# A router's rows turned by DMA transposes instead of TensorE, and a new order at the end of the attention

## The reference

```python
x = x + tanh(g_xattn[0]) * xattn(layernorm(x), ctx, ctx, ...)      # scores are abs(q k / 4), then softmax
x = x + tanh(g_ffn[0]) * ffn(layernorm(x), ...)

def ffn(x, w_router, w1, b1, w2, b2):
    xf = x.reshape(-1, 256)
    logits = xf @ w_router                                         # [4096, 8]
    probs = softmax(logits)
    topk_w, topk_idx = top_k(probs, 2)
    weights = sum(topk_w[..., None] * one_hot(topk_idx, 8), axis=1)
    h = gelu(einsum('te,ieh->tih', xf, w1) + b1)                   # 8 experts, 256 -> 1024
    out = einsum('tih,ihe->tie', h, w2) + b2                       # 1024 -> 256
    return sum(out * weights[..., None], axis=1)
```

## Time and profile before

| | |
|---|---|
| median of 3 runs | 665.48 us (664.07 to 665.98) |
| the profiled execution's own time | 665.24 us |
| its span, first to last instruction | 663.4 us |
| busy: PE / DVE / ACT / POOL | 638.7 / 459.6 / 334.2 / 312.5 us |
| mean granted TensorE clock | 0.982 of full speed |
| attention with router | from about 20 to 250 us |
| its end, mixed with the first expert tiles | from about 250 to 288 us |
| expert tiles of 256 rows, then of 128 | to 529 us, then to the end |

### The profile page before, as it was taken

The page is one execution under the profiler, slowest core; times in us unless marked ns, Lnnn a source line. Parts: engine busy times, 40 slices in busy tenths (PEclk is TensorE's granted clock), DMA queues, the critical chain, the costliest instruction groups (busy, mean ns, idle before and its releaser), DMA issues.

```text
span 663.4 us, 20913 instructions
## 1 busy us (share of the span) xinstructions
PE 638.7 (96%) x6637; PEld 565.5 (85%) x6638; DVE 459.6 (69%) x1298; ACT 334.2 (50%) x741; POOL 312.5 (47%) x420
## 2 busy tenths in 40 slices
PE   7899999999999998889999999999999999999992
PEld 6699999999999988778888888888888888888871
DVE  5688888888888885579756556564655647777772
ACT  4678778877887764532423333242332424444441
POOL 7323577777667553873443333243332434333332
PEclk9999999999999988799999999999999999999997
DMA  6143445554454463334764333333333334443322
GB/s 205 46 158 122 129 157 170 170 164 146 148 187 133 142 164 131 106 69 74 139 92 67 50 48 56 57 51 51 50 55 54 44 56 59 51 54 55 53 33 24
DMA packets 89157, 63.37 MB, mean 96 GB/s; under 512 B 51489, under 2 KB 84775, under 8 KB 88935
## 3 DMA queue, kind: packets, MB, share of 16 engines
q1 hardware_dynamic: 75519, 43.95, 25.6%
q0 software_dynamic: 13440, 18.14, 16.7%
q10 hardware_dynamic: 104, 0.04, 0.0%
HBM read 28.08 MB, written 24.63 MB: 79 GB/s over the span
## 4 chain that ended last, share of the span: by engine, by line
PE 52%; DVE 2%; POOL 2%; issue 1%; DMA 1%; ACT 0%; POOLq 0%; DVEq 0%; ACTq 0%
PE banks L1700 20%; PE banks L1683 19%; PE banks L1718 7%; PE banks L1732 7%; DMA out_dram<-prob_t,meta 1%; POOL routed L813 1%; DVE prob L1270 0%; POOL l_exp L794 0%; DVE v_area L1272 0%; ACT stage L970 0%; POOLq L676 0%; DVE prob_t L1287 0%; DVE prob_t L1283 0%; PE banks L1653 0%; POOL rstd L767 0%
## 5 line engine op out<-in xcount | busy, mean ns | idle before, releaser
L961 ACT ACTIVATE stage<-banks,bias_t 128x256 f32<-128x256 f32 x200 | 83.8, 470 | 166.3 <-PE banks L1683 166.2
L1683 PE MATMUL banks<-x_t,w_hi 128*128 128x256 f16 x800 | 135.6, 276 | 0.0
L1700 PE MATMUL banks<-w,prob 128*128 x800 | 132.4, 273 | 0.6 <-DVE v_area L1272 0.6
L850 POOL DMA_INDIRECT out_dram<-prob_t,meta x46 | 75.4, 1640 | 98.5 <-DVE prob_t L1262 86.7
L1683 PE MATMUL banks<-x_t,w_lo 128*128 128x256 f16 x400 | 110.6, 276 | 0.0
L1700 PE MATMUL banks<-w,v_area 128*128 x400 | 109.1, 273 | 0.0
L1683 PEld LDWEIGHTS banks<-x_t,w_hi 128*128 x800 | 79.1, 99 | 10.0
L1700 PEld LDWEIGHTS banks<-w,prob 128*128 128x128 f16 x800 | 78.0, 98 | 10.0 <-issue 0.8
L970 ACT ACTIVATE stage<-banks,bias_t 128x128 f32<-128x128 f32 x168 | 52.6, 363 | 66.8 <-PE banks L1718 66.5
L813 POOL DMA_INDIRECT routed<-row,pos x64 | 71.0, 1109 | 27.9 <-issue 14.7
L1612 PEld LDWEIGHTS banks<-v_area,prob_t 128*128 128x128 f32 x640 | 74.0, 192 | 4.3 <-DVE attn L1093 0.7
(11 more groups left out here) (244 smaller groups left out, 1262.3 us busy)
## 6 DMA issues: line engine op xcount, KB each, us to landing
stage<-in_L_ffn_w_dram SPq DMA_DIRECT2D x32, 512.0 KB, 4.3
x_in<-in_x_dram SPq DMA_DIRECT2D x16, 256.0 KB, 3.7
x_res<-in_x_dram SPq DMA_DIRECT2D x16, 256.0 KB, 4.1
out_dram<-x_res SPq DMA_DIRECT2D x16, 256.0 KB, 2.7
routed<-pad_rows SPq DMA_DIRECT2D x9, 265.0 KB
out_dram<-prob_t,meta POOLq DMA_INDIRECT x67, 3.8
routed<-row,pos POOLq DMA_INDIRECT x64, 2.8
arena<-in_L_ffn_b_dram SPq DMA_DIRECT2D x1, 1024.0 KB, 5.4
```

Of the source, the lines that this page charges most:

```text
L850: pool.indirect_dma_start(out[:, :], bass.IndirectOffsetOnAxis(ap=meta_of(j, pj)[:, b, E:E + 1].bitcast(U32), axis=0), y[:, pj, b], None, ...
L961: ins = act.activation(hid[:, c], H[:, q, c % PER * SLOTS:(c % PER + 1) * SLOTS], ACT.Gelu_apprx_tanh, bias=k.bias_t[:, bass.ds(e * HC + c ...
L1683: mm = pe.matmul(H[:, q, c % PER * SLOTS:(c % PER + 1) * SLOTS], w[:, bass.ds(e, 1), i, c * P:(c + 1) * P].rearrange("p a n -> p (a n)"), ...
L1700: mm = pe.matmul(Y[pj][:, b * D:(b + 1) * D], h[:, pj, c, b * P:(b + 1) * P], w[:, bass.ds(e, 1), c, :].rearrange("p a n -> p (a n)"), sta ...
```

## The change

For pairs 0 to 12 (`j < LAST_PAIRS`, 13 pairs) the router's rows are no longer turned by TensorE. SP issues two DMA transposes per pair, one per tile, from the fp16 halves in `row` (SBUF) to `rows_t` (SBUF), once both halves are written. `router_logits` then makes three fp16 products per chunk (high x high, high x low, low x high) with the router's weights, which are split into `router_hi` and `router_lo` once. It stands behind `turn_normalised` now. ACT's copy falls away for these pairs, and `copy_rows` and `turn_rows` stay for pairs 13 to 15, each with rows in a buffer of its own (`last_rows`, `x_in`), so that only the copy of pair 13 waits for a low half, that of pair 12.

Besides: the semaphore `router` counts 9 operations and `shared` the last three, `mask` and `l_shift` have two buffers, the padding rows are made at the end of the attention in the memory `turned` and written to DRAM later, `ident_bf` is a strided view of the fp32 identity, and the lists at the end of the attention are ordered anew on PE, ACT and DVE.

```diff
 # SP
                         sp.dma_start(x_res[:, (j - 1) % 2], x_rows[j - 1]).then_inc(x_res_ld[(j - 1) % 2], 16)
+                    if 0 <= j - 3 < LAST_PAIRS:
+                        turn_rows(j - 3)
+
+                def turn_rows(j):
+                    ready(sp, row_hi, j)
+                    ready(sp, row_lo, j)
+                    ready(sp, logit_ps, j - 1)
+                    for tile in range(2):
+                        sp.dma_start_transpose(rows_t[:, :, tile * P:(tile + 1) * P],
+                                               row[:, j % ROWS_HELD, tile, 0:D].bitcast(F16)).then_inc(rows_ld, 16)
...
 # ACT
                     ready(act, factors2, j, FACTOR_OPS[1])
-                    ready(act, logit_ps, j - 1)
+                    if j < LAST_PAIRS:
+                        ready(act, row_lo, j - 1)
+                    elif j == LAST_PAIRS:
+                        ready(act, q_ps, PAIRS - 1)
+                    else:
+                        ready(act, norm1, PAIRS - 1, 2)
...
                 def copy_rows(j):
-                    ready(act, x2t_ps, j)
-                    ready(act, row_lo, j)
+                    ready(act, x2t_ps, j - LAST_PAIRS)
+                    if j == LAST_PAIRS:
+                        ready(act, row_lo, j - 1)
...
-                    if exists(j - 3):
-                        copy_rows(j - 3)
...
-                e = expert(act, 0)
                 act.wait_ge(w_lo, 2 * PAIRS)
-                gelu(0, e, 0)
-                normalise_row(PAIRS - 2)
+                gelu(0, first, 0)
+                gelu(0, first, 1)
+                gelu(0, first, 2)
+                copy_rows(PAIRS - 2)
+                gelu(0, first, 3)
                 high_row(PAIRS - 2)
-                gelu(0, e, 1)
-                copy_rows(PAIRS - 2)
-                gelu(0, e, 2)
                 normalise_row(PAIRS - 1)
+                gelu(1, second, 0)
+                copy_rows(PAIRS - 1)
+                gelu(1, second, 1)
                 high_row(PAIRS - 1)
-                gelu(0, e, 3)
-                copy_rows(PAIRS - 1)
...
 # DVE, end of the attention
                 split_hidden(0, 0, 0)
-                low_row(PAIRS - 2)
+                split_hidden(0, 0, 1)
+                place_rows(PAIRS - 3)
+                shares(PAIRS - 3)
+                low_row(PAIRS - 3)
                 route(PAIRS - 2, 1)
                 choose(PAIRS - 2)
...
                 split_hidden(1, 1, 0)
                 place_rows(PAIRS - 1)
-                for q in range(1, HID_BANKS):
-                    split_hidden(1, 1, q)
+                split_hidden(1, 1, 1)
+                shares(PAIRS - 2)
+                low_row(PAIRS - 1)
+                split_hidden(1, 1, 2)
+                split_hidden(1, 1, 3)
+                finish_rows(0, 0, 0)
+                for q in range(HID_BANKS):
+                    split_hidden(2, 0, q)
                 shares(PAIRS - 1)
...
 # PE
                 def router_logits(j):
-                    ready(pe, x2t_sb, j)
                     ready(pe, places, j - 1, PLACE_OPS, 1)
+                    if j < LAST_PAIRS:
+                        ready(pe, router_halves, 0, 2)
+                        ready(pe, rows_ld, j, 32)
+                        for tile in range(2):
+                            n = 0
+                            for c in range(KC):
+                                for x, w in ((c, router_hi), (c, router_lo), (KC + c, router_hi)):
+                                    mm = pe.matmul(ROUTE[:, tile * E:(tile + 1) * E], rows_t[:, x, tile * P:(tile + 1) * P],
+                                                   w[:, c], start=(n == 0), stop=(n == 3 * KC - 1))
+                                    n += 1
+                        mm.then_inc(logit_ps, 1)
+                        return
+                    ready(pe, x2t_sb, j - LAST_PAIRS)
...
-                    if exists(j - 3):
-                        turn_rows(j - 3)
                     if exists(j - 2):
                         project_attention(j - 2)
+                    if j == PAIRS - 1:
+                        early_experts.extend(expert(pe, tile) for tile in range(2))
+                    if exists(j + 2):
+                        turn_normalised(j + 2)
                     if exists(j - 3):
                         router_logits(j - 3)
-                    if exists(j + 2):
-                        turn_normalised(j + 2)
...
+                first_layer(0, 0, 0, first, 0)
                 router_logits(PAIRS - 3)
                 turn_attention(PAIRS - 1)
-                first_layer(0, 0, 0, first, 0)
+                first_layer(0, 0, 0, first, 1)
                 project_attention(PAIRS - 1)
+                first_layer(0, 0, 0, first, 2)
                 ranks(PAIRS - 3)
-                first_layer(0, 0, 0, first, 1)
                 turn_rows(PAIRS - 2)
-                first_layer(0, 0, 0, first, 2)
+                first_layer(0, 0, 0, first, 3)
                 router_logits(PAIRS - 2)
-                first_layer(0, 0, 0, first, 3)
+                first_layer(1, 0, 1, second, 0)
+                first_layer(1, 0, 1, second, 1)
                 ranks(PAIRS - 2)
                 turn_rows(PAIRS - 1)
-                first_layer(1, 0, 1, second, 0)
-                first_layer(1, 0, 1, second, 1)
-                router_logits(PAIRS - 1)
                 first_layer(1, 0, 1, second, 2)
                 first_layer(1, 0, 1, second, 3)
+                router_logits(PAIRS - 1)
```

More of the change, by code:

```diff
@@ L544, in main_phase @@
         best_f = sb("best_f", [P, 2, 2])
-        mask = sb("mask", [P, 2, 2, E])
+        mask = sb("mask", [P, 2, 2, 2, E])
         weighed = sb("weighed", [P, 2, 2, E])
@@ L647, in small_meta, with normed @@
             return meta[:, p + 2 * (1 - b), 0]
+        def normed(j):
+            if j < LAST_PAIRS:
+                return x2_rows
+            return last_rows if j == LAST_PAIRS else x_in[:, j % 2]
         def row_halves(j):
@@ L1825, in _ @@
                 last = TILES - 1
-                first, second = expert(pe, 0), expert(pe, 1)
+                first, second = early_experts
                 score_banks_free(TILES)
```

137 lines of the change are left out of this document (73 added, 64 removed).

## The result

| | before | after |
|---|---|---|
| median | 665.6 us (664.07 to 665.98, 4 runs) | **676.48 us** (676.12 to 677.06, 4 runs) |
| ratio, 95% interval | | 1.0169 [1.0151, 1.0186] |
| the profiled execution's own time, span | 665.24, 663.4 us | 677.06, 675.2 us |
| mean granted TensorE clock | 0.982 | 0.974 |

A forecast was written before the change was run, and what follows sets the result against it. PE was taken to bound the kernel, each pair costing what PE issues. Pairs with the new wait +10.0, clock falls +13.6 and the end of the attention -8.0 gave +15.6 us on 665.24: 681 us, range 652 to 701.

The forecast's parts named there:

- Work that leaves PE, 0.94 us a pair: In each pair, fp32 transposes and logits (1.26 us) give way to 12 fp16 products (0.32 us): 13 pairs, 12.2 us less.
- The wait, 1.71 us a pair: Before the logits PE waits for the second DMA transpose, landing at 8.93 us; with PE's saving, +10.0 us over 13 pairs.
- the prediction's count: Time within a pair, counted from the end of the query projection on PE, where the attention's transposes begin.
- rival 3: Transposes collide with POOL's four scatters a pair and land at 4.5 us; wait 3.01 us, 706 us in all; chance 0.10.
- rival 1: Rows nearly in time: second transpose lands 2.1 us after its issue, 0.61 us waited a pair; 656 us; chance 0.24.
- DVE can't do those earlier: DVE's low halves of the rows cannot move forward, since operations before them hang on the same pair's query projection.
- the ring: Projection, ACT, DVE, SP, DMA, logits, then probabilities, scores, values, ranks, next projection: the wait comes back every pair.
- The clock, 8 falls of 1.7 us, +13.6 us: PE's granted clock falls behind the new wait in 8 of 13 pairs, at 1.7 us each: +13.6 us.
- Rival 2: The wait before the logits comes but PE's clock holds: +10.0 - 8.0, 667 us; chance 0.16.
- The end, -8.0 us: End of the attention: 4.6 of 5.0 us of PE's waits for ACT's copy and 3.4 us of clock falls go.
- SP's other issues at nothing: SP's rows out, x in and weight loads behind the transposes wait for DVE until 8.42 us anyway; costed at nothing.
- The rule that a transpose belongs on TensorE: A 128x128 transpose belongs on TensorE where a PSUM destination is acceptable; old form priced at 1.26 us a pair with logits.

The follow-up runs named there:

- stale: Changed kernel, but each pair's logits use the DMA transposes of the pair before, so PE does not wait for fresh rows; 645.71 us.
- early_low: Changed kernel with DVE computing the low halves of the rows right behind normalise_attn, about 1.2 us earlier; 654.0 us.
- early_late: Changed kernel with low halves 1.2 us earlier on DVE and the 12 products behind all three groups of probability transposes, ahead of the scores; 663.66 us.
- end_only: The change's order at the end of the attention alone; TensorE turns the rows and logits are fp32 in all 16 pairs, as before; 654.5 us.
- early3s: early3 with SP issuing the two transposes ahead of its load of x_res; 649.2 us.
- late: Changed kernel with the logits moved behind the transposes of the probabilities on PE; 676.92 us.
- mid: Changed kernel with the logits between the second and third group of the probabilities' transposes on PE; 666.08 us.
- early3: Changed kernel with DVE computing the rows' low halves ahead of the second weight split and the queries' low halves; 657.01 us.

## Why the prediction was right, and where it wasn't

- **Work that leaves PE, 0.94 us a pair:** right, 0.90 by stale, and the twelve products took 0.30 us against 0.32.
- **The wait, 1.71 us a pair:** right, 1.75. On the prediction's count from 145.10 the low halves end at 4.43 us (4.42 said), SP begins at 4.49, and the rows come at 9.38 instead of 8.93, while PE arrives a tenth or two later than the 7.22 said. The 3.2 us of the transposes from DRAM were a little short; what stretches the landing is a part of rival 3, POOL's scatters, at 0.55 us in the median and not 1.3. The 2.3 us that rival 1 sets beside its own 2.1 rest on a section of the Trainium skill (DMA: Bandwidth & Descriptors, Anatomy of one DMA) that is headed as GpSimd's path; these two are issued by SP, and in the median of the changed kernel the second was there some 3.4 us behind its own issue (4.59 less 1.2).
- **"DVE can't do those earlier":** wrong, though the sum did not rest on it. The operations in front of the low halves hang on the query projection, the low halves don't: their input was there at 144.16, 4.7 us before DVE took it. I read an order in a list as a dependence. This is the link of the ring that early_low cuts, and the 22 us it is worth are twice the loss that was to be explained.
- **The clock, 8 falls of 1.7 us, +13.6 us:** the size right, the make-up not. Four falls in the pairs, 1.5, 1.8, 1.7 and 5.0 us, and one in the head, 3.4 us: 13.4. The price of one was confirmed (1.62 us in early_late); the number was too high, the one of 5.0 us was not foreseen, and the fall in the head has no step in the prediction. In the pairs alone it was 10.0 us, so that the sum met 13.6 is luck. Rival 2, the clock holds, fell.
- **The end, -8.0 us:** right sign, mis-sized: -12.3 in this profile, -10.8 as a median by end_only. The waits went as taken (5.0 us to 1.1, and 0.67 us for DVE's mask besides); the term of the clock was 3.4 us and should have been up to 7.0, all that this stretch had lost. I had priced the falls from 260 to 285, took off only a part, and left out that the clock was already at 0.81 to 0.85 from 245 to 260.
- **SP's other issues at nothing:** right. The store of the rows starts at 153.53, 8.43 us on the count (8.42 said).
- **The rule that a transpose belongs on TensorE** (the Trainium skill, VectorE: DVE Perf Modes, Rules for kernel authors): for the change as it stands the rule was the better counsel, end_only being 22 us faster. With most of the landing covered it no longer looks so: early3s at 649.2 us, on the DMA, is 5 us under end_only at 654.5 by the medians, but their intervals overlap a little (up to 0.9784, from 0.9766 on), and the two were not timed beside each other.

**Open.** The fall in the head: the clock between 20 and 60 us was 0.91 in the kernel after, 1.00 in late and mid, 0.96 in stale, though all run the same head; the first logits came between 66.8 us (early3s) and 71.6 (early_late). So 3.4 of the 11.8 us may be an execution's luck. The kernel after was within 1 us in four runs, though its other three have a mean clock of 0.977 to 0.979 and not 0.974, and I can't tell. Nor is it known how much of the transposes' landing the weight load takes. That loaded code holds issue and landing is read from the times at which the packets start; no run moved them, and why a packet close behind the issue left the landing of the changed kernel as it was stays open.

## What to carry to other kernels

Before an engine's work is given to a DMA, write down when its source could be ready, when the list makes it ready, and when the reader arrives; the landing must fit between the last two, and an operation moved by one place on the producing engine can be worth more than the arithmetic saved (22 us here against 12). Then read each pair's landing, not the mean, and look at every queue beside it, that of the code too: early3 issued the transposes a microsecond earlier than early_low, its landings were up to two microseconds longer, and it lost 3 us by the medians. A short wait on TensorE counts at its own length plus a share of a fall. Filling it with idle products wins back the falls only; its own length is paid as before.

## What I had not expected of the hardware

- A wait of 0.47 us, the same in each pair, let the clock fall from 2.4 to 1.2 GHz in exactly every second pair of ten (clock 0.89 and 1.00 by turns), and each fall took 1.62 us.
- Two transposes of 128 KB each from SBUF to SBUF needed 4.0 us from the first issue to the reader's load with scatters starting 1.65 us behind them, 4.5 to 4.9 us with scatters starting 0.2 us before (medians 4.04 and 4.59).
- One 16 KB packet of loaded code beside them went with a landing of 6.0 to 7.0 us (seven pairs of early3 and early3s) instead of 4.4 to 4.9 (13 pairs), with the engines at 10 GB/s or less for 1.2 us (early3 at 123.89); in early_low the four pairs with such a packet are the four that wait. Read from the traces, not moved on purpose.
- A plain load of 256 KB issued 0.5 us before the transposes or right behind them made no difference to their landing (4.5 to 4.9 us in early3, 4.4 to 4.9 in early3s, in the pairs without a packet of code).
- The issue of a DMA transpose holds SP for 1.2 us as a rule and for up to 2.6 us now and then. In early_low the pairs in which it did so were those that still waited; in the kernel after two such pairs had their rows no later.
